# Linear attention between two mixture-of-experts layers: seven places in two written orders of work

## The chip, the cores and the metric

The kernel runs on one core of one Trainium2 chip. The metric is the device time of one execution in microseconds, median of the runs. A core has the engines TensorE (PE in the rows; PEld is its weight load), VectorE (DVE), ScalarE (ACT), GpSimd (POOL) and SyncE (SP), each with an instruction stream of its own that it executes in order; they wait for one another through semaphores.

## The reference, cut to what matters

```python
x = x + 0.5 * ffn(layernorm(x), router_w, w1, w2, bias)     # x is (8, 1024, 256), float32
x = x + attn(layernorm(x), w_qkv, w_gated, w_proj, gn_weight, gn_bias)
x = x + 0.5 * ffn(layernorm(x), router_w, w1, w2, bias)

def attn(x):                                  # 16 heads of 16
    q, k, v = split(x @ w_qkv.T)
    q, k = rope_xpos(q, k)
    scores = einsum('bhtd,bhsd->bhts', q, k) * 16 ** -0.5 * decay_mask
    y = einsum('bhts,bhsd->bhtd', scores, v)
    yn = (y - mean) / sqrt(var + eps) * gn_weight + gn_bias   # mean, var over (16, T) of a head
    return (silu(x @ w_gated.T) * yn) @ w_proj.T
# ffn: softmax(xf @ router_w), top 2 of 8 experts, capacity 1024 slots an expert, gelu between w1 and w2
```

## The kernel before

Three stages follow one another: the first expert layer with its routing, the attention, the second expert layer. The change touches the attention alone.

Attention works through 8 batches (b) of 8 tiles (n = 8 b + i) of 128 tokens. The causal product is computed in blocks of 64 tokens: `scores` and `attend` do the products inside a block, `new_state` adds k and v of a block to a running state in PSUM bank 7, and `memory` multiplies q by the state before the block. The decay is folded into the rotation tables, so that `mask` on VectorE only multiplies by a triangle.

TensorE's work comes in two kinds. Full blocks use the whole array of 128 x 128: `project` (q and k, L756), `project_values`, `gate`, `out_pair` (all L756), `turn` (transposes of a rotated tile, L812), `front_pair` (L774), `residual_pair` (L916), `head_means` (L887), `head_variances` (L895), `logits_back` (L955) and `counts` (L965, L966). Tiled blocks use a part of the array for each matmul: `new_state` (64 x 32, L827), `attend` (64 x 32, L877), `scores` (32 x 64, L844), `memory` (32 x 32, L862) and `logits` (128 x 32, L931).

Each engine has a function `sequence(b)`, which is called for b = -1 to 7 and lists the engine's steps in an order written out by hand; a step whose batch or tile does not exist falls away. Work of several batches is interleaved: b is in attention, b + 1 is being normalised and transposed (`front_...`), b - 1 is gated, projected and added to the rows (`gating`, `gated_low`, `out_pair`, `residual`), and the rows of b - 2 go through the choice of experts (`residual_pair`, `logits`, `logits_back`, `choice_part`, `counts`, `places`). So with b - 2 and b - 1 not there, b = 0 and 1 have shorter sequences.

What hangs together around the change:

- A tile n passes `project(n)` on TensorE (bank 0), `rotate(n)` on VectorE (L1805 to L1807), `rotated(n)` on GpSimd (L504), `turn(n)` on TensorE and `queries(n)` on ScalarE. There is one bank 0, so `project(n)` waits for `rotate(n - 1)`.
- `new_state(n, blk)` waits for the `carry` before it on VectorE (L1827), which copies the state out of bank 7; `carry(n, blk)` waits for `new_state(n, blk)`.
- `scores(n, phase)` fills banks 3 and 4 and waits until `mask` (L1817) has read the scores before it. `attend(n)` waits for both masks of n.
- Banks 1 and 2 are shared. A block takes one when the block before it in that bank has been copied out. In bank 2 come `turn`, `front_pair`, `residual_pair` and the gate's odd parts, in bank 1 the values (copied out by ScalarE, L1251), the gate's even parts, means, variances, logits and counts.
- `front_pair(b + 1, j)` is copied out by ScalarE (L1239, the high part) and then read by `front_low` on VectorE (L1791), which frees bank 2. `residual_pair` is copied out by ScalarE (L1339).
- The gate of batch b - 1: `gating` on VectorE (L1903, normalised output times gate) in two halves, `gated_high` on ScalarE (L1304), `gated_low` on VectorE (L1910), then `out_pair` on TensorE.
- The choice of batch b - 2: `logits`, ScalarE's copy, `logits_back`, `residual_choices` (from L1546), two `choice_part` and `places(0)` on VectorE, `counts` on TensorE, and `places(1)` on VectorE (L1579), which waits for `counts`.
- The group norm of b - 1 at the head of the sequence: `channels` (VectorE), `head_means`, `about_head` (VectorE, to L1876), `head_variances`.

The wait that the rotation sets is this line of `project`, and `carry` has its counterpart:

```python
if n >= 1:
    pe.wait_ge(A.qk_r, n)        # project(n): rotate(n - 1) has read bank 0
...
dve.wait_ge(A.st, 2 * n + blk + 1)   # carry(n, blk): new_state(n, blk) is in bank 7
```

Of the kernel before, what the change touches and what calls it, by code (L numbers as in the profile page):

```python
# [77 lines left out]
def macaron_kernel(nc, x_in, w_qkv, w_gated, w_proj, gn_w, gn_b, router_w, w1, w2, f_bias,  # L78
# [3 lines left out]
    with ctx:  # L82
# [500 lines left out]
        def _(pe):  # L583
# [297 lines left out]
            def head_means(b):  # L881

                if not 0 <= b < B:
                    return
                pe.wait_ge(A.gmv, b + 1)
                o, full = claim("means", b, 0)
                pe.matmul(o[:, 0:KC], headmean, gmv[:, :, 0], start=True, stop=True).then_inc(full, 1)  # L887
# [80 lines left out]
            def sequence(b):  # L968

                n = b * NT  # L970
                scores(n, 0)
                project_values(n + 1)
                project(n + 2)
                scores(n, 1)
                turn(n + 1)
                memory(n)
                new_state(n + 1, 0)
                head_means(b - 1)
                attend(n)
                residual_pair(b - 2, 2)  # L980
                scores(n + 1, 0)
                new_state(n + 1, 1)
                head_variances(b - 1)
                residual_pair(b - 2, 3)
                project(n + 3)
                project_values(n + 2)
                turn(n + 2)
                scores(n + 1, 1)
                new_state(n + 2, 0)
                logits(b - 2)  # L990
                memory(n + 1)
                logits_back(b - 2)
                scores(n + 2, 0)
                project(n + 4)
                attend(n + 1)
                new_state(n + 2, 1)
                scores(n + 2, 1)
                project_values(n + 3)
                turn(n + 3)
                memory(n + 2)  # L1000
                counts(b - 2)
                attend(n + 2)
                gate(b, 0)
                new_state(n + 3, 0)
                project(n + 5)
                scores(n + 3, 0)
                turn(n + 4)
                memory(n + 3)
                new_state(n + 3, 1)
                scores(n + 3, 1)  # L1010
                project_values(n + 4)
                gate(b, 1)
                out_pair(b - 1, 0)
                scores(n + 4, 0)
                attend(n + 3)
                new_state(n + 4, 0)
                scores(n + 4, 1)
                project(n + 6)
                project_values(n + 5)
                turn(n + 5)  # L1020
                new_state(n + 4, 1)
                gate(b, 2)
                new_state(n + 5, 0)
                project(n + 7)
                memory(n + 4)
                front_pair(b + 1, 0)
                new_state(n + 5, 1)
                attend(n + 4)
                scores(n + 5, 0)
                out_pair(b - 1, 1)  # L1030
                turn(n + 6)
                memory(n + 5)
                scores(n + 5, 1)
                project_values(n + 6)
                gate(b, 3)
                out_pair(b - 1, 2)
                attend(n + 5)
                front_pair(b + 1, 1)
                project_values(n + 7)
                new_state(n + 6, 0)  # L1040
                scores(n + 6, 0)
                out_pair(b - 1, 3)
                turn(n + 7)
                new_state(n + 6, 1)
                scores(n + 6, 1)
                project(n + 8)
                front_pair(b + 1, 2)
                memory(n + 6)
                scores(n + 7, 0)
                new_state(n + 7, 0)  # L1050
                project_values(n + 8)
                attend(n + 6)
                new_state(n + 7, 1)
                turn(n + 8)
                scores(n + 7, 1)
                new_state(n + 8, 0)
                project(n + 9)
                front_pair(b + 1, 3)
                memory(n + 7)
                attend(n + 7)  # L1060
                residual_pair(b - 1, 0)
                new_state(n + 8, 1)
                residual_pair(b - 1, 1)

            def drain():
# [23 lines left out]
            for b in range(-1, B):  # L1089
                sequence(b)  # L1090
# [354 lines left out]
        def _(dve):  # L1445
# [510 lines left out]
            def residual_shift(b):  # L1956
                if 0 <= b < B:
                    norm_shift(R[1], lnr, b)
# [8 lines left out]
            def sequence(b):  # L1967

                n = b * NT
# [21 lines left out]
                choice_part(b - 2, 0)  # L1991
                choice_part(b - 2, 1)
                places(b - 2, 0)
                gating(b - 1, 0)
                mask(n + 2, 1)
                carry(n + 2, 1)
                places(b - 2, 1)
                rotate(n + 4)
                gating(b - 1, 1)
# [48 lines left out]
                mask(n + 7, 1)  # L2048
                residual_shift(b - 1)
                carry(n + 8, 0)  # L2050
                rotate(n + 9)
                front_low(b + 1, 3)
                channel_stats(n + 6)
                carry(n + 8, 1)

# [128 lines left out]
```

## Time and profile before

| | |
|---|---|
| time, median of 3 runs | 2301.62 us (2299.54 to 2303.91) |
| the profiled execution | 2323.99 us, its span 2322.2 us |
| mean granted TensorE clock | 0.974 of full speed |
| first routing, to about 155 us | TensorE busy 106.8 us |
| first expert layer, 155 to 908 us | TensorE busy 749.4 us of 753 |
| attention, 908 to 1534 us | TensorE busy 566.8 us of 626 |
| second expert layer, 1534 us to the end | TensorE busy 759.2 us of 788 |
| instructions in attention | TensorE 12331 matmuls, VectorE 1246 operations |

The profile is one execution. Busy time is that of the engine, and a wait is idle time that ends when another engine releases the one that waits. The rows by stretch give the stretch, its length, then busy time and count of instructions of TensorE's matmuls, its weight loads, VectorE, ScalarE and GpSimd, the granted clock, the share of the DMA engines and GB/s. In a timeline the first number is the start in us from the span's start, the second the time, "x16" that 16 instructions are merged into one row, and what stands in brackets is the idle time before it and what ended it. Starts are exact, ends of matmuls are modelled. A few records of matmuls are missing, and a row may show fewer than the block has.

### The profile page before, as it was taken

How to read it: one execution, taken by the hardware profiler on the slowest of the kernel's cores; microseconds unless marked ns; L12 is line 12 of the kernel's file. 1: busy time of each engine (PE TensorE's matmuls, PEld its weight loads, DVE VectorE, ACT ScalarE, POOL GpSimd, SP SyncE). 2: the span in 40 equal slices, each digit the busy share in tenths (PEclk: the TensorE clock that was granted, in tenths of full speed). 3: DMA queues.
4: the chain of work that ended last, by engine and by line, in shares of the span. 5: the costliest groups of instructions: out<-in, count | busy, mean ns of one | idle time of the engine just before them, and what ended most of it. 6: DMA issues, size and time to landing. Idle time of an engine off the chain costs nothing.

```text
span 2322.2 us, 57931 instructions
## 1 busy us (share of the span) xinstructions
PE 2182.2 (94%) x22549; PEld 1919.0 (83%) x22549; DVE 1358.6 (59%) x3312; ACT 1003.4 (43%) x2149; POOL 1179.5 (51%) x911
## 2 busy tenths in 40 slices
PE   7869999999999997999999999849999999999998
PEld 6759999999999986777777777639999999999997
DVE  7755555555555552568878877545555555555553
ACT  4434434343434442445555555434343443444442
POOL 5765777735454533223344453354777754444443
PEclk9999999999999998999999999769999999999999
DMA  9523444434343424002211121123444443434432
GB/s 365 207 80 67 98 93 90 107 82 103 80 104 82 102 57 118 28 33 75 74 43 59 58 76 75 59 77 97 102 89 102 89 101 86 100 87 98 88 80 32
DMA packets 138440, 211.52 MB, mean 91 GB/s; under 512 B 34092, under 2 KB 114544, under 8 KB 132080
## 3 DMA queue, kind: packets, MB, share of 16 engines
q0 software_dynamic: 57344, 69.21, 18.2%
q1 hardware_dynamic: 80912, 139.72, 17.7%
q8 instruction: 132, 2.16, 0.4%
q14 instruction: 52, 0.43, 0.1%
HBM read 138.13 MB, written 72.88 MB: 91 GB/s over the span
## 4 chain that ended last, share of the span: by engine, by line
PE 52%; DVE 5%; issue 3%; ACT 1%; another core or an unknown queue 0%; POOL 0%; POOLq 0%; DMA 0%; DVEq 0%; ACTq 0%
PE bank L674 16%; PE bank L663 15%; PE bank L756 10%; PE bank L844 3%; PE bank L877 2%; PE bank L812 1%; PE bank L644 1%; PE bank L827 1%; PE bank L862 1%; PE bank L916 1%; PE bank L774 1%; DVE aw L1817 0%; DVE rt L1805 0%; DVE xnl L1791 0%; DVE lnr_mv L1458 0%
## 5 line engine op out<-in xcount | busy, mean ns | idle before, releaser
L1155 ACT ACTIVATE h<-bank 128x512 f32<-128x512 f32 x512 | 306.7, 599 | 858.1 <-PE bank L663 687.5
L1726 DVE CAST hh<-h 128x512 fp32r<-128x512 f32 x512 | 240.5, 470 | 700.0 <-ACT h L1155 621.2
L674 PE MATMUL bank<-w2h,hh 128*128 128x256 f32 x2048 | 582.3, 284 | 3.1 <-ACT yb L1173 3.1
L674 PE MATMUL bank<-w2h,hl 128*128 128x256 f32 x2048 | 579.5, 283 | 0.0
L674 PE MATMUL bank<-w2l,hh 128*128 128x256 f32 x2048 | 579.3, 283 | 0.0
L674 PEld LDWEIGHTS bank<-w2h,hh 128*128 128x128 f32 x2048 | 391.0, 191 | 22.3 <-ACT yb L1173 3.9
L663 PE MATMUL bank<-xh,w1h 128*128 128x512 f32 x1024 | 407.0, 397 | 1.7 <-DVE xl L1713 1.7
L663 PE MATMUL bank<-xl,w1h 128*128 128x512 f32 x1024 | 406.1, 397 | 0.0
L674 PEld LDWEIGHTS bank<-w2l,hh 128*128 128x128 f32 x2048 | 391.4, 191 | 16.4
L663 PE MATMUL bank<-xh,w1l 128*128 128x512 f32 x1024 | 400.2, 391 | 0.0
L674 PEld LDWEIGHTS bank<-w2h,hl 128*128 128x128 f32 x2048 | 391.2, 191 | 0.0
L461 POOL DMA_INDIRECT acc<-yb,tab x128 | 211.2, 1650 | 280.6 <-issue 209.1
L461 POOL DMA_INDIRECT out_rows<-yb,tab x128 | 211.4, 1652 | 280.0 <-issue 231.6
L1730 DVE TENSOR_TENSOR hl<-h,hh 128x512 fp32r<-128x512 f32 x512 | 350.3, 684 | 1.1
L394 POOL DMA_INDIRECT slot_table<-pay,idx x256 | 287.9, 1125 | 94.8 <-issue 80.0
L441 POOL DMA_INDIRECT xe<-xn_rows,rowtab x256 | 283.6, 1108 | 88.1 <-issue 77.1
L504 POOL TENSOR_TENSOR qk<-rt 128x512 f32<-128x512 f32 x64 | 88.5, 1382 | 293.4 <-DVE rt L1807 257.7
L663 PEld LDWEIGHTS bank<-xh,w1l 128*128 128x128 f32 x1024 | 193.6, 189 | 44.3
L663 PEld LDWEIGHTS bank<-xh,w1h 128*128 128x128 f32 x1024 | 195.5, 191 | 28.0 <-issue 2.3
L663 PEld LDWEIGHTS bank<-xl,w1h 128*128 128x128 f32 x1024 | 195.4, 191 | 22.1
L1173 ACT ACTIVATE yb<-bank,tab 128x256 f32<-128x256 f32 x256 | 100.7, 480 | 40.8 <-PE bank L674 40.8
L1817 DVE TENSOR_TENSOR aw<-bank,cst 128x512 f32<-128x512 f32 x128 | 87.9, 686 | 37.7 <-PE bank L844 36.3
(215 smaller groups left out, 3315.0 us busy)
## 6 DMA issues: line engine op xcount, KB each, us to landing
stg<-in_L_ffn_w SPq DMA_DIRECT2D x64, 1024.0 KB
xb<-acc SPq DMA_DIRECT2D x9, 1024.0 KB, 7.8
xa<-in_L_attn_x SPq DMA_DIRECT2D x8, 1024.0 KB, 13.9
xn_rows<-xa SPq DMA_DIRECT2D x8, 1024.0 KB
xn_rows<-xn_r SPq DMA_DIRECT2D x8, 1024.0 KB
xr<-acc SPq DMA_DIRECT2D x7, 1024.0 KB
out_rows<-xr SPq DMA_DIRECT2D x7, 1024.0 KB
slot_table<-pay,idx POOLq DMA_INDIRECT x256
```

The source lines that it names most:

```text
L394: pool.indirect_dma_start(out=slot_d[r], out_offset=bass.IndirectOffsetOnAxis(ap=idx[:, b, n:n + 1], axis=0), in_=pay_rows[:, b, 2 * n:2 * ...
L441: pool.indirect_dma_start(out=xe[j % 2][:, t, :], out_offset=None, in_=xn_d, in_offset=bass.IndirectOffsetOnAxis(ap=rowu[:, j, t, 0:1], ax ...
L461: pool.indirect_dma_start(out=dst, out_offset=bass.IndirectOffsetOnAxis(ap=tabu[:, j, t, 0:1], axis=0), in_=yb[j % 2][:, t, :], in_offset= ...
L504: pool.tensor_tensor(qk[:, n % 2, :], rt1[:, n % 2, :], rt2[:, n % 2, :], ALU.add).then_inc(A.roped, 1)
L663: last = pe.matmul(bank[fj % 2][:], a[:, k, w], c[j % 2][:, k, :], start=(n == 0), stop=(n == 5))
L674: last = pe.matmul(o, a[:, fj, s], c[:, fj, :], start=(fj == 0 and n == 0 and (end or t % 2 == 0)), stop=(fj == FJ - 1 and n == 2), skip_g ...
L756: last = pe.matmul(out, a(k), c(k), start=(n == 0), stop=(n == 3 * KC - 1))
L1155: act.activation(h32[fj % 2][:], bank[fj % 2][:], ACT.Gelu_apprx_tanh).then_inc(f.gelu, 1)
L1173: act.activation(yb[j % 2][:, t, :], tile_sum(j, t, end), ACT.Copy, scale=tab[:, j, t, 1:2]).then_inc(f.y, 1)
L1726: dve.tensor_copy(hh[:, fj, :], h32[fj % 2][:]).then_inc(f.hh, 1)
L1730: dve.tensor_tensor(hl[:, fj, :], h32[fj % 2][:], hh[:, fj, :].bitcast(fp32), ALU.subtract).then_inc(f.hl, 1)
L1817: dve.tensor_tensor(aw[:, n % 2, phase].rearrange("p x h m q -> p x (h m) q"), banks[:, 3:5, 0:2 * P].rearrange("p x (m q) -> p x m q", m= ...
```

## The change

On TensorE, inside `sequence(b)`: `scores` of the next batch's first tile moves from the head of the sequence to the end of the one before, between `new_state(n + 8, 1)` and `residual_pair(b - 1, 1)`; `residual_pair(b - 2, 2)` moves ahead of `attend(n)`; `scores(n + 2, 0)` ahead of `logits_back`; `attend(n + 2)` ahead of `counts`; `project(n + 5)` ahead of `new_state(n + 3, 0)`; `gate(b, 2)` ahead of `new_state(n + 4, 1)`; and `project(n + 7)` ahead of `new_state(n + 5, 0)`. On VectorE, `gating(b - 1, 0)` moves behind `mask(n + 2, 1)` and `carry(n + 2, 1)`, and `front_low(b + 1, 3)` ahead of `rotate(n + 9)`. No step is added or taken away, and no wait inside a step changes.

```diff
--- before.py
+++ after.py
@@ -968,7 +968,6 @@
             def sequence(b):
 
                 n = b * NT
-                scores(n, 0)
                 project_values(n + 1)
                 project(n + 2)
                 scores(n, 1)
@@ -976,8 +975,8 @@
                 memory(n)
                 new_state(n + 1, 0)
                 head_means(b - 1)
+                residual_pair(b - 2, 2)
                 attend(n)
-                residual_pair(b - 2, 2)
                 scores(n + 1, 0)
                 new_state(n + 1, 1)
                 head_variances(b - 1)
@@ -989,8 +988,8 @@
                 new_state(n + 2, 0)
                 logits(b - 2)
                 memory(n + 1)
+                scores(n + 2, 0)
                 logits_back(b - 2)
-                scores(n + 2, 0)
                 project(n + 4)
                 attend(n + 1)
                 new_state(n + 2, 1)
@@ -998,11 +997,11 @@
                 project_values(n + 3)
                 turn(n + 3)
                 memory(n + 2)
+                attend(n + 2)
                 counts(b - 2)
-                attend(n + 2)
                 gate(b, 0)
+                project(n + 5)
                 new_state(n + 3, 0)
-                project(n + 5)
                 scores(n + 3, 0)
                 turn(n + 4)
                 memory(n + 3)
@@ -1018,10 +1017,10 @@
                 project(n + 6)
                 project_values(n + 5)
                 turn(n + 5)
+                gate(b, 2)
                 new_state(n + 4, 1)
-                gate(b, 2)
+                project(n + 7)
                 new_state(n + 5, 0)
-                project(n + 7)
                 memory(n + 4)
                 front_pair(b + 1, 0)
                 new_state(n + 5, 1)
@@ -1060,6 +1059,7 @@
                 attend(n + 7)
                 residual_pair(b - 1, 0)
                 new_state(n + 8, 1)
+                scores(n + 8, 0)
                 residual_pair(b - 1, 1)
 
             def drain():
@@ -1991,9 +1991,9 @@
                 choice_part(b - 2, 0)
                 choice_part(b - 2, 1)
                 places(b - 2, 0)
-                gating(b - 1, 0)
                 mask(n + 2, 1)
                 carry(n + 2, 1)
+                gating(b - 1, 0)
                 places(b - 2, 1)
                 rotate(n + 4)
                 gating(b - 1, 1)
@@ -2048,8 +2048,8 @@
                 mask(n + 7, 1)
                 residual_shift(b - 1)
                 carry(n + 8, 0)
+                front_low(b + 1, 3)
                 rotate(n + 9)
-                front_low(b + 1, 3)
                 channel_stats(n + 6)
                 carry(n + 8, 1)
 
```

## Rows read from the trace of the kernel before

**Rows 1.** Busy time by stretch: the attention stage alone.

```profile
908.00:1534.00 626.00, 566.83 (x12331) 448.67 (x12331) 456.31 (x1246) 329.04 (x628) 226.08 (x178) 0.94 0.18 64
```

**Rows 2.** TensorE's waits, attention stage: us in total, times, longest.

```profile
PE bank L877 <- DVE aw L1817: 6.2, 6, 1.1
...
PE bank L916 <- ACT xrT L1339: 4.5, 8, 0.8
...
PE bank L916 <- DVE xnl L1791: 4.1, 4, 1.0
```

**Rows 3.** Timeline, TensorE, batch 5 (columns: start us, us): tiled between full.

```profile
1301.24 0.40 PE L756 MATMUL bank<-xnh,wTl 128*128 128x512 f32 x1
1301.48 0.40 PE L756 MATMUL bank<-xnl,wTh 128*128 128x512 f32 x1
1301.81 0.33 PE L827 MATMUL bank<-vz,qk 64*32 64x32 f32 x16
1302.07 0.50 PE L756 MATMUL bank<-wTh,xnh 128*128 128x512 f32 x1
1302.41 0.39 PE L756 MATMUL bank<-wTl,xnh 128*128 128x512 f32 x1
```

**Rows 4.** The same view, batch 0: two tiled blocks of one mode in succession.

```profile
940.29 0.32 PE L827 MATMUL bank<-vz,qk 64*32 64x32 f32 x15
940.43 0.24 PE L877 MATMUL bank<-aw,vz 64*32 64x64 f32 x1
```

**Rows 5.** The same view, batch 5, TensorE and VectorE: logits_back to scores(n+3, 1).

```profile
1291.80 0.44 PE L955 MATMUL bank<-cst,lg 128*128 128x128 f32 x2
...
1292.34 0.21 DVE L1546 TENSOR_REDUCE red<-bank 128x8 f32<-128x64 f32 x1
...
1297.49 1.20 DVE L1903 TENSOR_TENSOR yg<-yg,gT 128x1024 f32<-128x1024 f32 x1
...
1297.81 0.39 PE L965 MATMUL bank<-scn,cst 128*128 128x16 f32 x2
...
1298.61 0.69 DVE L1817 TENSOR_TENSOR aw<-bank,cst 128x512 f32<-128x512 f32 x1
...
1299.44 0.85 PE L877 MATMUL bank<-aw,vz 64*32 64x64 f32 x64 [1.02 <-DVE aw L1817]
...
1300.56 0.41 DVE L1807 TENSOR_TENSOR rt<-bank,rope 128x256 f32<-128x256 f32 x1
...
1302.35 2.79 DVE L1910 TENSOR_TENSOR ygl<-yg,ygh 128x1024 fp32r<-128x1024 f32 x1
...
1305.89 0.72 PE L844 MATMUL bank<-qm,qkT 32*64 32x128 f32 x16
```

**Rows 6.** Groups by line (busy us, mean ns), attention stage: gated_low.

```profile
L1910 DVE TENSOR_TENSOR ygl<-yg,ygh 128x1024 fp32r<-128x1024 f32 x14 | 33.1, 2365 | 0.0
```

**Rows 7.** Timeline, end of batch 5's sequence: ScalarE, VectorE and TensorE.

```profile
1344.51 0.60 ACT L1239 ACTIVATE xnh<-bank 128x512 fp32r<-128x512 f32 x1 [0.47 <-PE bank L774]
...
1344.52 0.68 DVE L1805 TENSOR_TENSOR rt<-bank,rope 128x512 f32<-128x512 f32 x1
...
1345.78 0.68 DVE L1791 TENSOR_TENSOR xnl<-bank,xnh 128x512 fp32r<-128x512 f32 x1
...
1346.61 0.63 PE L916 MATMUL bank<-cst,xn_r 128*128 128x128 f32 x4 [1.01 <-DVE xnl L1791]
```

**Rows 8.** The same view, end of the first sequence (b = -1).

```profile
935.48 0.60 ACT L1239 ACTIVATE xnh<-bank 128x512 fp32r<-128x512 f32 x1 [0.97 <-PE bank L774]
...
937.03 0.40 PE L756 MATMUL bank<-wTh,xnh 128*128 128x512 f32 x1
```

**Rows 9.** The same view, head of batch 1: head_variances on TensorE.

```profile
1005.84 0.38 PE L895 MATMUL bank<-gsm,cst 128*128 128x2 f32 x2 [0.46 <-DVE gsm L1876]
```

**Rows 10.** The same view, middle of batch 5: copy of bank 1, then the gate.

```profile
1314.86 0.38 ACT L1251 ACTIVATE vz<-bank 128x256 f32<-128x256 f32 x1 [3.45 <-PE bank L756]
...
1315.45 0.50 PE L756 MATMUL bank<-xnh,wTh 128*128 128x512 f32 x1
```

## The prediction, made before the changed kernel ran

> **What bounds the kernel now.** I read the busy time by stretch first. The edits lie in the attention stage alone, 626 us of the 2322.2 us span, and there TensorE is busy for 566.8 us, VectorE for 456.3, ScalarE for 329.0 and GpSimd for 226.1 [rows 1]. TensorE carries the stage, so each us taken from it counts, as long as what it waits for keeps up. The granted clock is 0.94 there, so some of it ran at the lower of its two levels [rows 1]. Then I read TensorE's waits. Three kinds come back in batch after batch: `attend` for a mask on VectorE (6 times, 6.2 us), a residual turn for ScalarE's copy out of bank 2 (8 times, 4.5 us), and a residual turn for the low part `front_low` on VectorE (4 times, 4.1 us) [rows 2]. Last I read the timeline of single batches beside the four orders written in the code, and measured TensorE's blocks from start to start, because the ends of matmuls are modelled. A reader should see there that VectorE is idle for a quarter of the stage and still ends TensorE's waits: its order is fixed, so an operation that waits holds all that stand behind it.
>
> **What the moves on TensorE save.** Between two full matmuls of 512 columns the step is 0.24 us. Before a tiled block it is 0.33, the block takes 0.26, and the first full matmul behind it takes 0.34 [rows 3]. An edge between full and tiled therefore costs 0.1 us. Counting the written order with the operations that exist in each batch, 408 such edges become 328, since each of 40 moves (per batch b = 2 to 6 six of them, in b = 0 two) turns full, tiled, full, tiled into full, full, tiled, tiled: 80 x 0.1 = 8.0 us less TensorE time.
>
> Two tiled blocks of one mode overlap: the second starts 0.14 us behind the first [rows 4], where the same block takes 0.26 us ahead of a full one [rows 3]. The moved blocks become neighbours of another tiled mode, so by that rule a move saves one drain and not two: 40 x 0.12 (0.26 less 0.14) = 4.8 us in place of 8.0. The trace agrees that a mode of its own matters, and the sum goes by the rows.
>
> **The seam of two batches (b = 1 to 6).** VectorE started the rotation at 1344.52 and `front_low` only at 1345.78, though ScalarE's copy was done at 1344.51 + 0.60 = 1345.11. `residual_pair(b - 1, 0)` started at 1346.61, 0.15 behind the end of the low part, after a wait of 1.01 us [rows 7]. With the low part first it starts some 0.05 behind the copy, ends at 1345.84, and the pair starts at 1345.99: 0.6 us earlier. `scores(n + 8, 0)`, moved between the two residual pairs, then lies in the wait for ScalarE's copy, about 0.55 us each time [rows 2], and two edges go (0.2). That is 1.4 us. Not all arrives. At the head of the next batch `head_variances` follows a chain on VectorE (statistics, mask, rotation, `about_head`) whose first step waits for ScalarE's copy of the last output; in batch 1 TensorE was already 0.46 us late there for it [rows 9]. Also `residual_pair(b - 2, 2)`, moved ahead of `attend(n)`, loses the 0.8 us that attend covered while ScalarE empties bank 2 of `turn(n + 1)`, and will wait nearly 0.5 us. I take 0.9 us for b = 2, 4, 5, 6, and 0.5 for b = 1 and 3, where the long wait is missing (4 times, not 6 [rows 2]): -4.6 us, with bounds 0 and 6 x 1.4 = -8.4.
>
> **The two seams before these.** They have no residual pair to help, and the rotation is late all the same. At b = -1 the copy ended at 935.48 + 0.60 = 936.08; then low part (0.68), rotation (1.26 to its successor [rows 7]) and 0.2 of handing over give 938.2 for `project(2)`, which started at 937.03 [rows 8]: +1.2 us. At b = 0 the chain to `head_variances` slips by nearly the same, and that one has no slack [rows 9]: +0.9. Bounds 0 and +1.3 each.
>
> **From the logits to the gate's low part (b = 2 to 7).** In this stretch three moves meet. Before, `logits_back` started at 1291.80 and `scores(n + 3, 1)` at 1305.89, 14.1 us later [rows 5]. After, in us behind the old place of `logits_back`:
> - It stands behind `scores(n + 2, 0)`, so it starts at 0.6; the maximum on VectorE follows 0.5 later, 1.1 (before: 0.54).
> - From there to the end of `places(0)` VectorE needs as before 1297.49 - 1292.34 = 5.15: 6.25. Now the mask comes, not the product of 1.20, and `attend(n + 2)` follows 0.83 behind the mask's start: 7.1 (before: 7.64).
> - `counts` now stands behind attend (0.8): 7.9, and its four matmuls are out at 8.5. `places(1)` waits for them and the rotation of n + 4 stands behind it; before, that ended at 1300.56 + 0.41, which is 1.67 behind the mask's end (1298.61 + 0.69): now about 10.2.
> - `project(n + 5)`, ahead of `new_state(n + 3, 0)`, waits for this rotation, 10.35 (it wanted to start some 0.6 earlier). The new state follows at 11.85 (1.5).
> - `carry(n + 3, 0)` waits for the new state, and behind it stand `gated_low` and `mask(n + 3, 0)`. The low part started 1302.35 - 1301.81 = 0.54 behind the new state [rows 3, 5]: 12.4. It took 2.79 in that batch [rows 5] and 2.37 in the mean [rows 6]; it overlapped a GpSimd rotation sum there, which now ends about when it starts, so I take 2.25. `scores(n + 3, 1)` came 0.75 behind its end: 15.4.
> So +1.3 us (+1.9 with 2.79). The cause is one: `new_state(n + 3, 0)` is pushed back by a projection of 1.5 us, and the longest VectorE operation of the batch hangs on it. This price includes the edges saved there. For b = 2, 3, 5, 6 I take 1.3; for b = 4 and 7, where scores waited a little more before, 1.1; for b = 1, which has the gate's product but no logits, 1.0; b = 0 has neither and gains 0.2. Sum: 5.2 + 2.2 + 1.0 - 0.2 = +8.2 us, bounds +3 and +12. The product itself, moved behind the mask, delays ScalarE's copy of it by 1.3 us; the low part starts that much later anyway.
>
> **The gate in the middle (all eight).** `gate(b, 2)` wants to start two edges and a state earlier, but its bank 1 is copied out until 1314.86 + 0.38 = 1315.24 and it already started at 1315.45 [rows 10]; 0.15 behind the copy it gains 0.06 of the 0.4 it wants. The states behind it then cost their 0.26 again: +0.1 each, +0.8 in all, bounds -2 and +1.
>
> **Sum.** -4.6 + 1.2 + 0.9 + 8.2 + 0.8 = +6.5 us. The profiled execution took 2323.99 us, 1.8 outside its span, and the median of the timed runs is 2301.62, 1% less; I add the sum unscaled: 2308.
>
> **Rivals.**
> - TensorE alone decides: the chains have slack that I don't see, and the time falls by 8.0 (edges) + 4 x 0.6 (low part) + 6 x 0.55 (copy) = 13.7 us: 2288. For it: TensorE is busy nine tenths of the stage [rows 1]. Against: every one of the waits in rows 2 is ended by a chain of this kind. With half of the chain's price absent, it comes out at about 2298. Chance of both 0.13.
> - The skill's rule alone, with each chain as slack: 4.8 us less and the seams' 5.7, 2291; it has part of the chance above, 0.03.
> - Gain and loss cancel: the longer waits lie over instruction-fetch waits of TensorE, or the low part is shorter than 2.25: 2301 to 2306. Chance 0.27.
> - The forecast, slower by 5 to 9 us: 0.48. It decides from the point where `new_state(n + 3, 0)` starts more than 0.2 us later than before, since `scores(n + 3, 1)` follows it at a fixed distance.
> - The same with TensorE's clock: more and longer gaps (1.2 + 0.6 + 1.2 us within ten) bring one or two more stretches at the lower level; a stretch of 7 us of work at half speed is worth 3 us: 2311 to 2316. Chance 0.12.
>
> **How the numbers follow.** The measurement tells about 0.2% (4.6 us) from no change. Slower by more: 0.48 + 0.12 = 0.60. Within: 0.27. Faster: 0.13. The range runs from the half-absent chain, 2298, to the case of the clock, 2314.
>
> **What the profile after would show.** `scores(n + 3, 1)` (L844) waits for VectorE by over 1 us in batches 1 to 7, and the line of `gated_low` starts 1 us or more later relative to `turn(n + 3)`. `project(n + 5)` waits for the rotation by about 0.6. The wait of L916 for `xnl` shrinks to 0.4 or less, and the one for `xrT` goes. `project(2)` in the first sequence waits for a rotation by 1.2. TensorE's matmul and load counts are the same. If L844 shows no such wait, the forecast is wrong and the first rival holds; if `head_variances` starts 1.4 and not 0.9 us earlier in its batch, the seam is worth 3 us more.

## The result, and the profile after

The changed kernel takes 2320.54 us in the median, the kernel before 2301.62 beside it: a ratio of 1.008, 95% interval 1.0067 to 1.0093. One of the changed kernel's five executions took 4129.33 us and is left out of the ratio; the other four lie between 2316.16 and 2324.8 with a median of 2318.9. That is slower, as forecast, but by 18.9 us (17.3 by the median of the four) instead of 6.5, and outside the range of 2298 to 2314. The profiled execution took 2324.8 us with a span of 2323.0.

One thing has to be known first. The kernel before runs at two paces: with a median of about 2302 us beside the changed kernel and beside e1 to e8, of 2319 to 2321 us beside e9 to e16. What sets the pace is not known; the chip alone does not, since e5 to e8 and e9 to e12 ran on the same one. All ratios below are taken within one pace. The profiled execution of before that stands ahead of the prediction (2323.99 us) is of the slower pace, the times beside it are of the faster. So I took a second trace of before at the faster pace (e5: 2304.49 us, span 2302.7), and the trace of the changed kernel is compared with that one.

The attention stage by stretch, start to end of TensorE's work in it, e5 first, then the kernel after (columns as in rows 1):

```profile
903.00:1514.00 611.00, 557.69 (x12330) 442.68 (x12330) 457.73 (x1245) 328.16 (x626) 224.87 (x176) 0.95 0.19 66
```

```profile
903.00:1534.00 631.00, 559.99 (x12328) 445.95 (x12328) 457.28 (x1245) 326.66 (x625) 226.14 (x176) 0.95 0.18 64
```

The same work, the same busy time within 2.3 us, 20 us more length, and the same mean clock of 0.95: what the 80 edges saved is more than eaten up by idle time. Those of TensorE's waits in the attention stage of the kernel after that bear on the change (us in total, times, longest):

```profile
PE bank L877 <- DVE aw L1817: 7.3, 7, 1.2
PE bank L844 <- DVE aw L1817: 6.0, 7, 1.0
...
PE bank L827 <- issue: 3.8, 3, 1.9
PE bank L895 <- DVE gsm L1876: 3.8, 6, 1.2
PE bank L877 <- issue: 3.4, 4, 1.3
PE bank L756 <- DVE base L1581: 3.4, 6, 0.6
...
PE bank L916 <- ACT qm L1263: 2.1, 6, 0.4
...
PE bank L916 <- ACT xrT L1339: 1.3, 2, 0.8
PE bank L756 <- DVE rt L1807: 1.0, 1, 1.0
```

Against rows 2: `attend` still waits for the mask; `scores` (L844) now waits 7 times too; `residual_pair` no longer waits for ScalarE's copy 8 times but 2, and in its place wait `head_variances` (L895, 6 times), `residual_pair` for `queries` (L1263, 6 times), and a gate for `places` (L1581, 6 times). "issue" is idle time that no engine ends; it is called a stop below.

The length of each part, summed over b = 1 to 7 from the starts of the blocks, after less e5, in us:

| part of the sequence | after less e5 | forecast |
|---|---|---|
| start to the first `turn(1)` of attention | +1.3 | +1.2 |
| batch 0, `turn(1)` to `turn(9)` | +3.2 | -0.1 |
| head of a batch, `turn(n+1)` to `head_variances` | +3.5 | with the end of a batch |
| `memory(n+1)` to `turn(n+3)` | -1.2 | in the next |
| `turn(n+3)` to `scores(n+3,1)` | +10.7 | +8.4 with the line above |
| `turn(n+5)` to `turn(n+6)`, the middle | +6.5 | +0.7 |
| end of a batch, `attend(n+7)` to `turn(n+9)` | -4.8 | -3.7 with the head |
| everything else | +0.9 | 0 |
| sum | +20.1 | +6.5 |

Single stretches at the low clock are in these figures on both sides. In the kernel after one stands in the head of batch 0, which is 1.8 us longer, nearly all of it by this (granted clock 0.82), and one behind `head_variances` in batch 1, 1.5 us (0.68, in e5 1.00); e5 has one in the head of batch 5 (0.75), 1.6 us, and these last two cancel in "everything else".

### The profile page after: what moved, and what is told of

The parts are those of the page before. It is cut to its first block, busy times and chain, and to the rows that moved or that the text cites. A ratio compares the mean times of both kernels' runs of the same rounds, so it can differ in the third digit from the quotient of the medians.

```text
span 2323.0 us, 57931 instructions
## 1 busy us (share of the span) xinstructions
PE 2172.6 (94%) x22549; PEld 1916.1 (82%) x22549; DVE 1361.4 (59%) x3312; ACT 1002.5 (43%) x2149; POOL 1166.7 (50%) x911
## 4 chain that ended last, share of the span: by engine, by line
PE 51%; DVE 6%; issue 3%; ACT 1%; POOL 0%; DMA 0%; POOLq 0%; DVEq 0%; ACTq 0%
PE bank L674 16%; PE bank L663 15%; PE bank L756 9%; PE bank L844 3%; PE bank L877 1%; PE bank L644 1%; PE bank L812 1%; PE bank L827 1%; PE bank L862 1%; PE bank L916 1%; DVE aw L1817 1%; PE bank L774 1%; DVE rt L1805 0%; DVE d L1501 0%; DVE lnr_mv L1458 0%
## 5 line engine op out<-in xcount | busy, mean ns | idle before, releaser
L394 POOL DMA_INDIRECT slot_table<-pay,idx x256 | 281.5, 1100 | 89.9 <-issue 80.0
L504 POOL TENSOR_TENSOR qk<-rt 128x512 f32<-128x512 f32 x64 | 88.6, 1384 | 301.5 <-DVE rt L1807 272.0
L1722 DVE TENSOR_TENSOR w2l<-stg,w2h 128x256 fp32r<-128x256 f32 x256 | 105.2, 415 | 0.0
```

The costliest lines, as they stand in the source:

```text
L394: pool.indirect_dma_start(out=slot_d[r], out_offset=bass.IndirectOffsetOnAxis(ap=idx[:, b, n:n + 1], axis=0), in_=pay_rows[:, b, 2 * n:2 * ...
L504: pool.tensor_tensor(qk[:, n % 2, :], rt1[:, n % 2, :], rt2[:, n % 2, :], ALU.add).then_inc(A.roped, 1)
L1722: dve.tensor_tensor(w2l[:, fj, :], stg2[:, fj, :], w2h[:, fj, :].bitcast(fp32), ALU.subtract).then_inc(f.w2l, 1)
```

## The experiments

Differences in us are the ratio times 2302 or 2320. Each edit is one against the kernel before.

**The projection alone (e1), and all without it (e2).**

```diff
                 gate(b, 0)
+                project(n + 5)
                 new_state(n + 3, 0)
-                project(n + 5)
```

> The kernel before with one move alone: project(n + 5) ahead of new_state(n + 3, 0). Theory 1 (a chain on VectorE): new_state(n + 3, 0) starts 1.4 us later in each batch, carry, gated_low and mask(n + 3, 0) hang on it, and scores(n + 3, 1) waits about 0.8 us more in batches 1 to 7: +5 us. Theory 2 (TensorE's time alone counts): one pair of mode edges less in each of 8 batches, -1.6 us. Theory 3 (most of the +18.9 us of the whole change lies outside these chains, in TensorE's instruction supply or its clock, and comes with any move that puts tiled blocks side by side): the move alone costs more than 8 us.

> The whole change without the move of project(n + 5). Theory 1: the new state starts earlier, but the rotation behind places(1) still ends 1 us later than before and gating and carry stand behind it, so that scores(n + 3, 1) is still about 0.7 us late in batches 2 to 7; with the gain of the seams and the loss of the first two: +2 to +4 us against the kernel before. Theory 2: the same as the whole change less 1.6 us, so +20 against before. Theory 3: between +10 and +18.

Measured: e1 1.0017 [1.0004, 1.0029], +3.9 us; e2 1.0068 [1.0053, 1.0083], +15.6. In e1 `turn(n+3)` to `scores(n+3,1)` grows from 9.18 us to 9.8 to 10.0 in batches 2 to 7, by a wait of `scores` for the mask (6.1 us, 7 times). The two add up to the whole, so the projection is a fifth of the loss and the rest lies elsewhere. Cut finer the parts do not add up: e1, e3, e4 and e8 come to 22.5 us. Why the projection and e8 overlap is told with the main term below.

**The seam alone (e3).** `scores(n + 8, 0)` at the end, `residual_pair(b - 2, 2)` ahead of `attend(n)`, `front_low(b + 1, 3)` ahead of `rotate(n + 9)`.

> The kernel before with the edits at the seam of two batches alone: scores of the next batch between the two residual pairs, residual_pair(b - 2, 2) ahead of attend(n), front_low(b + 1, 3) ahead of rotate(n + 9). Theory 1: -4.6 at six seams, +2.1 at the first two: -2.5 us. Theory 2: -8 us. Theory 3: slower than before by over 4 us.

Measured: 1.0001 [0.9992, 1.001]. Nothing is gained. In batches 2 and 4 the end is 0.95 us shorter (6.66 to 5.71) and the head of the next batch 0.90 longer (`turn(n+1)` to `head_variances` 3.97 to 4.87); in batches 3 and 6, where `attend` has a stop of 0.5 us in the head of e5, the head is 0.2 longer. The waits of e3:

```profile
PE bank L895 <- DVE gsm L1876: 3.1, 6, 1.2
...
PE bank L916 <- ACT qm L1263: 2.1, 6, 0.4
```

Summed over the batches, from the starts in e3 and e5: -5.1 us at the ends, +3.3 at the heads, +1.2 ahead of attention's first turn, and +1.5 for a stretch at the low clock behind `head_variances` in batch 1 (granted clock 0.69). The timeline of the seam of batch 5 in the kernel after:

```profile
1352.29 0.69 DVE L1791 TENSOR_TENSOR xnl<-bank,xnh 128x512 fp32r<-128x512 f32 x1 [2.00 <-ACT xnh L1239]
...
1353.12 0.63 PE L916 MATMUL bank<-cst,xn_r 128*128 128x128 f32 x4
...
1353.94 0.67 PE L844 MATMUL bank<-qm,qkT 32*64 32x128 f32 x16
...
1356.13 0.49 DVE L1837 BATCH_NORM_STATS2 gst<-yT 128x6 f32<-128x128 f32 x2 [0.77 <-ACT yT L1276]
...
1357.84 0.66 PE L812 MATMUL bank<-cst,qk 128*128 128x128 f32 x4
...
1360.00 0.63 PE L916 MATMUL bank<-cst,xn_r 128*128 128x128 f32 x4 [0.36 <-ACT qm L1263]
...
1362.48 0.16 DVE L1876 SCALAR_TENSOR_TENSOR gsm<-gmv,gsm 128x2 f32<-128x2 f32 x1
...
1362.69 0.38 PE L895 MATMUL bank<-gsm,cst 128*128 128x2 f32 x2 [0.36 <-DVE gsm L1876]
```

and the same place in e5:

```profile
1335.31 0.42 DVE L1807 TENSOR_TENSOR rt<-bank,rope 128x256 f32<-128x256 f32 x1
1335.64 0.68 DVE L1791 TENSOR_TENSOR xnl<-bank,xnh 128x512 fp32r<-128x512 f32 x1
...
1336.47 0.63 PE L916 MATMUL bank<-cst,xn_r 128*128 128x128 f32 x4 [0.33 <-ACT xn_r L1105]
...
1337.87 0.63 PE L916 MATMUL bank<-cst,xn_r 128*128 128x128 f32 x4 [0.52 <-ACT xrT L1339]
```

In e5 the low part was done at 1336.32 and the pair started at 1336.47, 0.15 behind it as in rows 7, after a wait of 0.33 us and not of 1.01. The view puts this wait down to ScalarE's normalised rows, whose second two were done at 1336.38; but in the kernel after the pair starts at 1353.12, ahead of the end of the same two, so it does not need them, and the 0.33 us are the low part's as well. Moving the low part up wins 0.2 us of them (`attend(n+7)` to `residual_pair(b-1,0)`: 1.19 to 0.99). The wait of 1.01 us is in every trace of the slower pace (4 times, 4.0 to 4.1 us) and in none of the faster one. There the pause of VectorE ahead of it stands in the timeline of before at the same seam:

```profile
1344.38 0.23 DVE L1827 TENSOR_TENSOR state<-bank,cst 128x64 f32<-128x64 f32 x1 [1.46 <-remote]
```

**The middle: both moves (e4), the same with TensorE's instructions shifted (e6, e7), each move alone (e9, e10).** e4 moves `gate(b, 2)` ahead of `new_state(n + 4, 1)` and `project(n + 7)` ahead of `new_state(n + 5, 0)`. e6 is e4, and e7 the kernel before, with this ahead of attention:

```diff
+            for n in range(128):
+                pe.wait_ge(S0.const, 16)
```

> The kernel before with the two moves in the middle of a batch alone: gate(b, 2) ahead of new_state(n + 4, 1), project(n + 7) ahead of new_state(n + 5, 0). Theory 1: the gate waits for its bank, +0.8 us. Theory 2: -1.6 us. Theory 3: the gap without a releaser inside attend(n + 4), 0.2 to 1.7 us in the changed kernel's trace, comes with these two moves, +6 us.

> The kernel before, once more, for a second trace. Its first trace (span 2322.2 us) is 20 us over the median of the timed runs, and the other runs so far show the seam of two batches, from attend(n + 7) to turn(n + 9), at 6.65 us where they leave it as it was and not at the 7.34 of the rows read for the prediction. If the first trace was not typical, this one has a span near 2300 and a seam of 6.65 us with a wait of L916 for the low part under 0.5 us; if it was typical, 7.34 and 1.0.

> The kernel of e4 (the two moves in the middle of a batch) with 128 satisfied waits on TensorE ahead of the attention stage, which shift every later instruction in TensorE's stream by half of a 16 KB piece. Theory of instruction supply: the gaps inside attend(n + 4) (1.2 to 1.9 us in batches 2, 3, 5, 6) vanish or move to other blocks, and the time differs from e4 by 2 us or more either way, most likely -4. Rival (the gaps belong to the blocks themselves, a memory or a mode of the array): gaps at the same blocks, time as e4, 0.4% over before.

> The kernel before with the same 128 satisfied waits ahead of the attention stage. Theory of instruction supply: the two gaps at batch ends (1.8 and 3.2 us) leave their blocks and others appear, so that a kernel with the same work on every engine changes by up to 6 us, more likely slower, since the order before has few gaps. Rival: no change, under 1 us.

> Only gate(b, 2) moves ahead of new_state(n + 4, 1). In the run with both moves of the middle the stretch from memory(n + 4) to turn(n + 6) grew from 4.2 us to 4.6 to 7.4 us. Theory A, the projection does it: project(n + 7) ahead of new_state(n + 5, 0) makes that state 1.2 us later, and carry(n + 5, 0), slot_entries and front_low(b + 1, 0) on VectorE hang on it; then gate(b, 2) alone costs next to nothing, 2301 to 2303 us against 2301.8, and memory(n + 4) to turn(n + 6) stays at 4.2. Theory B, each move brings half, through the bunching of tiled blocks and the gaps of instruction fetch: 2304 to 2306, with gaps that no engine ends inside attend(n + 4).

> Only project(n + 7) moves ahead of new_state(n + 5, 0); new_state(n + 4, 1) stays ahead of gate(b, 2). Theory A (the projection does it): 2306 to 2310 us, nearly the whole +7 us of both moves, turn(n + 6) waits for front_low(b + 1, 0), and the gaps inside attend(n + 4) are there. Theory B (each half): 2304 to 2306.

Measured: e4 1.004 [1.0026, 1.0054], +9.2 us; e6 1.0031 [1.0015, 1.0048] against e7 0.9989 [0.9978, 0.9999], so 0.42% between them; e9 1.0025 [1.0006, 1.0044], +5.8; e10 1.0014 [1.0003, 1.0025], +3.2. Theory A, that the projection does it all, has fallen: each move costs, and the two parts add up to the whole within their intervals. Shifting the instructions moves the stops (below) but not the price. The traces put the price where the moves are: beside the trace of before of the same pace, `turn(n+5)` to `turn(n+6)` over all eight batches is 7.7 us longer in e9 and 2.0 in e10, 9.7 together. Three things are seen. In e9, `turn(n+5)` to `memory(n+4)` grows from 4.24 us to 4.93 to 5.06, with a wait of L827 for the carry (3.1 us, 7 times). In e4 the stretch from `memory(n+4)` to `turn(n+6)` grows from 4.21 us to 7.4 in batch 2, 5.9 in batch 5 and 4.6 to 4.7 in three others. First the small excess, of which this is batch 4 in e4:

```profile
1240.12 0.23 DVE L1827 TENSOR_TENSOR state<-bank,cst 128x64 f32<-128x64 f32 x1 [1.78 <-PE bank L827]
...
1243.63 1.67 DVE L1651 TENSOR_SCALAR sel<-sel 128x16 f32<-128x16 f32 x1
...
1243.97 1.29 POOL L504 TENSOR_TENSOR qk<-rt 128x512 f32<-128x512 f32 x1
...
1245.56 0.69 DVE L1791 TENSOR_TENSOR xnl<-bank,xnh 128x512 fp32r<-128x512 f32 x1
...
1246.40 0.63 PE L812 MATMUL bank<-cst,qk 128*128 128x128 f32 x4
```

and in e5:

```profile
1239.83 0.18 DVE L1651 TENSOR_SCALAR sel<-sel 128x16 f32<-128x16 f32 x1
...
1239.93 1.28 POOL L504 TENSOR_TENSOR qk<-rt 128x512 f32<-128x512 f32 x1 [1.16 <-PE bank L827]
...
1240.12 1.13 DVE L1654 TENSOR_TENSOR idx<-sel 128x16 uint32<-128x16 f32 x1
...
1241.29 0.69 DVE L1791 TENSOR_TENSOR xnl<-bank,xnh 128x512 fp32r<-128x512 f32 x1
...
1242.47 0.60 PE L812 MATMUL bank<-cst,qk 128*128 128x128 f32 x4
```

`turn(n+6)` takes bank 2, which the low part frees: in e4 it starts 0.15 us behind the low part's end, in e5 0.49 behind. On VectorE `carry(n+4,1)` waits 1.78 us for the state that was moved back, and one small operation took 1.67 us instead of 0.18. That operation ends at 1245.30, 0.04 us behind GpSimd's rotation sum (1243.97 + 1.29); in e5 another small one (L1654) takes 1.13 us and ends 0.04 behind the same sum. So the same neighbour costs more here: from L1648 (1243.43, in e5 1239.63) to the low part it is 2.13 us instead of 1.66. The large excess is a stop of TensorE inside `attend(n+4)`. In batch 2 of e4 a stretch at the low clock is added to it (0.77 over these 7.4 us). In the kernel after, batch 2, the stop looks like this:

```profile
1108.50 0.81 PE L877 MATMUL bank<-aw,vz 64*32 64x64 f32 x59
1110.45 0.30 PE L877 MATMUL bank<-aw,vz 64*32 64x64 f32 x4 [1.14 <-issue]
```

and this is all that the DMA engines moved from 1107.9 to 1109.2 us:

```profile
q8 instruction: 1, 0.02, 5.1%
```

The block stops after 60 of its 64 matmuls, waits for no engine, and goes on 1.1 us later; what went before is one packet of the instruction queue. So it is throughout: in the nine traces of the faster pace all 69 stops of 0.4 us or more between 930 and 1480 us end 2.2 to 3.0 us behind the start of such a packet, and such packets start 4.7 us apart in the mean. And the moves bring more of the stops, shifted or not: 11.5 us of them in e4 against 8.5 in e5, 12.1 in e6 against 7.6 in e7.

**Between the logits and the low part (e8, e11, e14, e15).** e8 has `scores(n + 2, 0)` ahead of `logits_back`, `attend(n + 2)` ahead of `counts` and the product behind mask and carry. e15 has the first of these alone, e14 the last alone:

```diff
-                gating(b - 1, 0)
                 mask(n + 2, 1)
                 carry(n + 2, 1)
+                gating(b - 1, 0)
                 places(b - 2, 1)
                 rotate(n + 4)
```

e11 is e15 with the product moved two steps further, behind `rotate(n + 4)`.

> The kernel before with the three edits at the choice of experts alone: scores(n + 2, 0) ahead of logits_back, attend(n + 2) ahead of counts, gating(b - 1, 0) behind the mask and carry on VectorE. Chain theory: VectorE starts the choice 0.5 us later and places(1), the rotation behind it and the low part of the gate 1 us later, so from turn(n + 3) to scores(n + 3, 1) 1.1 us more and 0.2 less ahead of it: +0.9 in batches 2 to 7, +5.4 us. Theory that TensorE's time alone counts: -2.5 us.

> Of the moves between the logits and the gate's low part only scores(n + 2, 0) ahead of logits_back is kept; counts stays ahead of attend(n + 2) and project(n + 5) behind new_state(n + 3, 0). gating(b - 1, 0) moves further on VectorE, behind places(b - 2, 1) and rotate(n + 4). The theory of the chain: in us behind the old place of logits_back, places(0) ends at 6.25, the mask at 6.95, carry at 7.1, places(1) and the rotation end at 8.7 to 8.9 instead of 9.2; attend(n + 2) starts at 7.1 instead of 7.64. new_state(n + 3, 0) then starts 0.3 to 0.5 us earlier than before. The low part needs the product and ScalarE's copy of it, which now start 1.2 us later than before or more; if it is late by more than new_state is early, scores(n + 3, 1) pays. So: -0.5 us in each of five or six batches where the low part keeps up, 2298 to 2300; 0 to +0.5 where it does not, 2301 to 2304. The rival that the three moves are bad one by one, whatever VectorE's order: 2304 or more.

> Only gating(b - 1, 0) moves behind mask(n + 2, 1) and carry(n + 2, 1) on VectorE. attend(n + 2) no longer waits 1.0 us for the mask. The chain theory: the low part starts when gating(b - 1, 1) is done, 0.2 us earlier at most, and mask(n + 3, 0) and scores(n + 3, 1) follow it, so the wait of 1 us moves to scores(n + 3, 1): turn(n + 3) to scores(n + 3, 1) stays at 9.0 to 9.2 us and the ratio is 0.999 to 1.000. The rival, that TensorE's own waits count one by one: 6 x 1.0 us less, ratio 0.997.

> Only scores(n + 2, 0) moves ahead of logits_back(b - 2). The chain theory: the steps of the choice on VectorE start 0.6 to 0.7 us later, and with them the mask, both products, the low part and mask(n + 3, 0), so scores(n + 3, 1) comes 0.4 to 0.7 us later in b = 2 to 7: +2.5 to +4 us, ratio 1.001 to 1.002. The rival, edges alone: two edges less in each of six batches, -1.2 us, ratio 0.9995.

Measured: e8 1.004 [1.0025, 1.0056], +9.2 us; e14 1.0003 [0.9988, 1.0018]; e15 1.0028 [1.0014, 1.0043], +6.5; e11 1.0087 [1.007, 1.0104], +20.

e14 is the cleanest test of the chain. The wait of `attend` for the mask (6.2 us, 6 times) is gone, and these stand in its place:

```profile
PE bank L756 <- DVE base L1581: 3.7, 6, 0.6
...
PE bank L844 <- DVE aw L1817: 3.0, 7, 0.5
```

```profile
1302.05 0.86 PE L877 MATMUL bank<-aw,vz 64*32 64x64 f32 x64
...
1303.56 0.47 PE L756 MATMUL bank<-xnh,wTh 128*128 128x512 f32 x1 [0.65 <-DVE base L1581]
...
1305.85 2.92 DVE L1910 TENSOR_TENSOR ygl<-yg,ygh 128x1024 fp32r<-128x1024 f32 x1
...
1308.70 0.68 DVE L1817 TENSOR_TENSOR aw<-bank,cst 128x512 f32<-128x512 f32 x1
...
1309.52 0.67 PE L844 MATMUL bank<-qm,qkT 32*64 32x128 f32 x16 [0.45 <-DVE aw L1817]
```

`turn(n+3)` to `scores(n+3,1)` is 9.13 us against 9.18: 6 us of waits taken away won nothing. `new_state(n+3,0)` starts 0.4 us earlier, but VectorE has the same two products to do ahead of the low part, which starts 0.20 earlier (5.46 behind `turn(n+3)` instead of 5.66) and takes 2.92 us instead of 2.78; mask and scores follow its end. In e11 the low part came late (7.40 us behind `turn(n+3)` instead of 5.66) though TensorE had `new_state(n+3,0)` ready 0.4 us earlier than before, and `scores(n+3,1)` waited 1.5 us. I had reckoned with half a us at most. The loss of 20 us is that of the rival, but not by its reason: the chain is 0.8 us longer a batch, 4.6 in six, and the larger part comes behind it, as follows.

e15 cost twice what its chain explains. In batch 2 `memory(n+1)` to `scores(n+3,1)` is 0.5 us longer, as expected, in batches 3 to 6 it is 1.9. The rows show why (batch 5, behind the old wait of `attend`, now 1.19):

```profile
1304.29 1.17 PE L877 MATMUL bank<-aw,vz 64*32 64x64 f32 x64 [1.19 <-DVE aw L1817]
...
1305.99 0.63 PE L756 MATMUL bank<-xnh,wTl 128*128 128x512 f32 x1
...
1307.63 0.39 PE L756 MATMUL bank<-xnl,wTh 128*128 128x512 f32 x1
```

```profile
1304.00:1307.40 3.40, 3.11 (x69) 2.58 (x70) 2.93 (x8) 2.37 (x3) 1.48 (x1) 0.52 0.20 31
```

The granted clock is 0.52 there, the lower of the two levels (1.2 of 2.4 GHz), and a matmul of 512 columns takes 0.63 us instead of 0.40. `gate(b, 0)` to the next state takes 2.56 us there and 1.57 in e14, 1.0 us more, and 1.0 to 1.3 more in each of batches 3 to 6. In e8 the gate ran so in four batches. In its trace the chain costs 5.3 us, as forecast (0.9 in each of six batches), the clock at these gates another 3.7 (0.93 each), and a low stretch behind `head_variances` in batch 1 another 1.5: 10.5 for the 9.2 timed. In e11 such stretches stand behind the wait of `scores` (granted clock 0.78 over batch 5's), together with some stops of 0.3 to 0.5 us, where `scores(n+3,1)` to `turn(n+5)` grew from 8.8 us to 13 or 14 in batches 3 to 6.

**A seam that gains (e12, e13), and both gains together (e16).** Of the seam's moves only `scores(n + 8, 0)` is kept. On ScalarE the output copy of the last tile moves from the head of the next sequence to the end of this one:

```diff
                 residual_evac(b - 1, 0)
+                if b < B - 1:
+                    output(n + 7)
                 residual_evac(b - 1, 1)
```

e13 is this alone, e12 this on top of e11, e16 this on top of e14.

> As the kernel with counts first, and at the seam only scores(n + 8, 0) moves to the end of the sequence, with residual_pair(b - 2, 2) and front_low(b + 1, 3) where they were; on ScalarE output(n + 7), until now the first step of the next sequence, moves between the two residual copies at the end of this one. The seam alone won 0.95 us at the end of a sequence and lost 0.92 at the head of the next, where head_variances waited for a chain on VectorE that begins behind ScalarE's copy of the last output. If that chain is the cause, the copy comes about 0.7 us earlier here, the head keeps its old length, and the time is 3 to 6 us below the kernel with counts first. If the head is bound by something else, the two come out within 1.5 us of each other.

> Only the seam: scores(n + 8, 0) at the end of the sequence and on ScalarE output(n + 7) between the two residual copies; everything else as before. If the head of the next batch hangs on the chain behind ScalarE's output copy, the end of each sequence of b = 1 to 6 is 0.7 us shorter and the head keeps its length (turn(n + 1) to head_variances 4.0 us): 6 x 0.7 = 4 us less, a ratio of 0.998 (0.997 to 0.999). If the head is bound otherwise, it takes the 0.7 back: ratio 1.000.

> The seam of the kernel with the earlier output copy and the product behind the mask together. The two do not share a chain, so the gains should add: ratio 0.997 to 0.998 by the chain theory (-4 us and -1 us), 0.995 if TensorE's waits count one by one. If stretches at the low clock move with the gaps, it can come out up to 3 us to either side.

Measured: e12 1.0036 [1.002, 1.0052], which is 0.5% below e11; e13 0.998 [0.9966, 0.9994]; e16 0.9976 [0.9963, 0.9988]. In e13 the end of each batch is 0.7 us shorter (7.34 to 6.59 in batch 2), and the heads stay at 3.97 where TensorE has no stop of its own. The wait of `head_variances` is what it was in e5:

```profile
PE bank L895 <- DVE gsm L1877: 0.5, 1, 0.5
```

So the head hangs on the chain behind the output copy, as the forecast said. e13 alone would not tell this, as it also leaves `residual_pair(b - 2, 2)` behind `attend(n)`; the timeline of the kernel after does, where VectorE's statistics (1356.13) wait 0.77 us for that copy and `head_variances` (1362.69) for the end of the chain that starts with them. And e16 is 0.24% faster than the kernel before. e12 won more against e11 than the 3 to 6 us expected; its trace has 11 stretches at the low clock where e11 has 16, and I did not separate that part.

## Why the prediction was right or wrong

**The sign and the main term were right, its single cause was not.** Logits to low part: forecast +8.2 us with `scores(n+3,1)` 1.3 late in a batch. Measured: `memory(n+1)` to `scores(n+3,1)` is 1.2 us longer in each of batches 3 to 7, 0.95 in batch 1, and 2.5 in batch 2, where `gate(b, 0)` fell into a stretch at the low clock: 9.5 in all. The timeline of batch 5 after, which answers rows 5:

```profile
1303.71 0.85 PE L877 MATMUL bank<-aw,vz 64*32 64x64 f32 x64 [1.16 <-DVE aw L1817]
...
1305.35 0.17 DVE L1581 TENSOR_TENSOR base<-bank,base 128x16 f32<-128x16 f32 x1
...
1305.67 0.47 PE L756 MATMUL bank<-xnh,wTh 128*128 128x512 f32 x1 [0.57 <-DVE base L1581]
...
1308.63 0.33 PE L827 MATMUL bank<-vz,qk 64*32 64x32 f32 x16
...
1309.17 2.03 DVE L1910 TENSOR_TENSOR ygl<-yg,ygh 128x1024 fp32r<-128x1024 f32 x1
...
1311.10 0.70 DVE L1817 TENSOR_TENSOR aw<-bank,cst 128x512 f32<-128x512 f32 x1
...
1311.95 0.67 PE L844 MATMUL bank<-qm,qkT 32*64 32x128 f32 x16 [0.97 <-DVE aw L1817]
```

The low part starts 0.54 behind the state, as in rows 3 and 5, and takes 2.03 us, where I took 2.25; `scores` follows at 0.75 behind its end, as I had it. The state is 1.9 us later than before, where I had 1.84. One wait was put in the wrong place: the forecast let `project(n+5)` wait 0.6 us for the rotation. It is `gate(b, 0)` that waits 0.57, because it takes bank 1 from `counts`, which `places(1)` (L1581) must read first. When the gate is through, the rotation is done (1306.78, the gate at 1307.14). The sum is the same.

"The cause is one" was wrong. Without the projection, in e8, `scores(n+3,1)` is still 0.9 us late in a batch; the projection alone (e1) makes it 0.65 late, both together 1.2. They do not add up because of the length of the low part: it takes 2.03 us where GpSimd's rotation sum (L504) is over before it starts (e1, after), 2.78 where they overlap by 0.9 us (e5), and 2.93 where they overlap by 1.1 (e2, e8). A later low part is a shorter one, so a projection that delays it by 1.2 to 1.4 us costs half of that or less.

Of the signs named, `scores` waits in batches 1 to 7 (6.0 us, longest 1.0) where over 1 us was forecast, `project(2)` by 1.0 instead of 1.2, the wait for the low part at the seam is gone, and that for ScalarE's copy is down from 8 times to 2.

**The first seam was right.** `project(2)` waits 1.0 us for a rotation [rows 8 gave +1.2]; +1.25 us up to the first turn.

**The seam of two batches failed.** With the first two seams, e3 was to win 2.5 us (-4.6 + 2.1); it won nothing. In the kernel after ends and heads of a batch come to -1.4 us where the forecast has -3.7. Two steps failed. The 0.6 us for the earlier low part rested on rows 7, which are of a pace that the timed runs did not have; it is worth 0.2. (The other 0.75 us, for `scores` in the wait for ScalarE's copy and two edges, is exact: `residual_pair(b-1,1)` to `turn(n+9)` 4.06 to 3.30.) And of 1.4 us that the end of a batch was to gain, I let a third be lost at the head of the next; of the 0.95 that it gains, 0.90 are lost where the head had no stop before, and 3.5 of 4.8 us in all in the kernel after. The chain was named ("whose first step waits for ScalarE's copy of the last output"), and priced with the slack of rows 9 of one batch; in e5 the chain ends at 1345.78 and `head_variances` would start at 1345.91 (3.97 behind `turn(n+1)`), so it has 0.1 us of slack. With that copy earlier (e13) the 0.75 us arrive.

**The middle failed by its size.** The forecast was +0.8 with a bound of +1; it measures +7.9 in the traces (6.5, and 1.4 in batch 0) and +9.2 timed in e4. The term priced was `turn(n+5)` to `memory(n+4)`: 0.1 a batch forecast, 0.17 measured. What was put at nothing is all that stands behind it, `memory(n+4)` to `turn(n+6)`: 6.5 of the 7.9 us, in TensorE's stops inside the next tiled blocks (three of 0.9 to 1.3 us in the kernel after and two of 0.5) and in the low part that frees bank 2 (0.2 to 0.4 in a batch). I priced the moved step and did not follow what the moved states release on VectorE, which I had done for the other moves.

**The clock rival had part of the truth.** It was given 3 us. In the kernel after, batch 2 shows it (1.3 us), and so do the heads of batches 0 and 1, but the stage as a whole has the same mean clock in e5, so it is no part of the 20 us in sum. In e15 it is most of the loss in each of batches 3 to 6 (1.4 of 1.9 us).

**The edges.** Where nothing waits behind them, they are worth what rows 3 say: in e15 and e8 `memory(n+1)` to `turn(n+3)` is 0.20 us shorter (5.47 to 5.27), two edges at 0.1; in e10 `turn(n+5)` to `memory(n+4)` 0.20 (4.24 to 4.04).
**What stays open.** Why VectorE pauses 1.46 us at four seams at one pace and not at the other, and what sets the pace. And what in the two moves of the middle brings the stops in `attend(n+4)`: that stops go with the packets of the instruction queue and that these moves bring more of them is shown; that the bunched tiled blocks are the reason is only argued, and e3 and e8, which bunch such blocks too, have 4.6 and 9.1 us of stops against 8.5 in e5.

## What to carry to other kernels

In this kernel an order with fewer changes between full and tiled blocks won 0.1 us an edge only where the step that is pushed back releases nothing; follow each moved state through the engine that it releases up to the next bank that this engine frees. Where a long operation on another engine stands ahead of a mask, that engine's order sets the pace: moving TensorE's steps or taking its waits away (e14) wins nothing there, and one block of TensorE moved together with the one copy at the head of the chain (e13) wins what the three moves of e3 did not. The releaser that a view names is the last of several, not always the one that was needed: compare the starts in two traces, as at the seam. Before a term rests on a wait of 1 us, see whether the profiled execution runs at the pace of the timed ones: here it was 1% longer, and the wait belonged to that 1%.

## What the runs showed of the hardware that I had not expected

- TensorE stops for 0.4 to 1.9 us with no engine to wait for (e5, after), in or ahead of tiled blocks for the most part, and goes on 2.2 to 3.0 us behind the start of a packet of the instruction queue. With 128 instructions more ahead of attention (e6, e7) the stops stand at other places: 4.8 us in four stops of `attend` in e7 against 1.0 us in two in e5, at a time that is not longer (0.9989).
- A wait of 1.2 us ahead of `attend(n+2)` was followed by a gate at a granted clock of 0.5 to 0.75 in five of six batches of e15, four of e8 and one of the kernel after; it costs another 0.7 to 1.3 us on the gate's 1.6. A gap can so cost twice. What decides is not settled: e8 and the kernel after have the same pair of waits there (1.16 and 0.57 us).
- Operations of VectorE on up to 16 elements a partition can be held by an addition on GpSimd. L1651, L1652 and L1654 take 0.16 to 0.18 us when GpSimd's rotation sum (L504) does not run beside them and up to 1.67 us when it does. In the 18 traces all 341 operations of that size that took over 0.8 us between 930 and 1480 us end within 0.05 us of the end of an addition on GpSimd, 339 of them of L504. The low part of the gate (128x1024) is longer by the same neighbour: 2.03 us alone, 2.92 with 1.1 us of overlap.
